# Conditioned layer norm: VectorE reads scale and bias in PSUM, without ScalarE's copies

## What is computed

```python
cond = silu(emb @ f_w1 + f_b1) @ f_w2 + f_b2          # (256, 16), from noise levels
for i in range(4):
    # y = layernorm(x) * (1 + cond @ s1_w[i] + s1_b[i]) + (cond @ b1_w[i] + b1_b[i])
    y = cond_layer_norm(x, cond, s1_w[i], s1_b[i], b1_w[i], b1_b[i])
    x = x + sparse_attention(y, src, dst, wq[i], ..., wo[i], bo[i])
    y = cond_layer_norm(x, cond, s2_w[i], s2_b[i], b2_w[i], b2_b[i])
    x = x + relu(y @ m_w1[i] + m_b1[i]) @ m_w2[i] + m_b2[i]
```

## Time and profile before

| | us |
|---|---|
| median of 3 runs | 902.3 (902.26 to 905.46) |
| the profiled execution, its own time | 895.13 |
| span of its trace | 893.3 |
| PE busy | 777.2 |
| DVE busy | 607.8 |
| ACT busy | 230.4 |
| POOL busy | 139.3 |
| mean granted clock of PE | 0.954 |

### The profile page before, as it was taken

How to read it: one execution, slowest core, us unless ns; L and a number is a source line. 1 busy time by engine, 2 the same in 40 slices (tenths; PEclk the granted TensorE clock), 3 DMA queues, 4 the chain that set the end, 5 groups by cost and what they waited for, 6 DMA issues and landing times.

```text
span 893.3 us, 10417 instructions
## 1 busy us (share of the span) xinstructions
PE 777.2 (87%) x2858; PEld 499.2 (56%) x2858; DVE 607.8 (68%) x1579; ACT 230.4 (26%) x460; POOL 139.3 (16%) x149
## 2 busy tenths in 40 slices
PE   6688898898898999999999997188979995996998
PEld 2345465455466657657558563176566582582673
DVE  8774675675684533533633544288999999999895
ACT  6522122123122321321321221401602403403300
POOL 6000000000001000000010001741261261240000
PEclk9889999999999999999999999599999997997999
DMA  6813214323331333333233100671541452330000
GB/s 203 293 40 114 102 55 150 106 79 121 106 118 40 121 111 113 106 112 112 105 112 107 59 0 23 192 227 51 169 139 47 142 142 71 100 113 0 0 1 23
DMA packets 39653, 89.93 MB, mean 101 GB/s; under 512 B 3986, under 2 KB 4255, under 8 KB 39615
## 3 DMA queue, kind: packets, MB, share of 16 engines
q1 hardware_dynamic: 34496, 72.71, 24.3%
q0 software_dynamic: 5120, 16.78, 6.4%
HBM read 88.43 MB, written 1.05 MB: 100 GB/s over the span
## 4 chain that ended last, share of the span: by engine, by line
PE 33%; issue 32%; DVE 23%; DVEq 7%; POOL 2%; ACT 1%; DMA 1%; POOLq 0%; ACTq 0%; SPq 0%
PE PS L744 23%; DVE big L1446 6%; PE PS L1003 5%; DVE tail L1437 5%; DVEq L1416 3%; DVE tail L1456 2%; DVE prods L1456 2%; PE PS L753 2%; DVEq L1420 1%; POOL rstd L537 1%; DVEq L1446 1%; POOL big L557 1%; DVE h L1088 1%; PE PS L840 1%; PE PS L777 1%
## 5 line engine op out<-in xcount | busy, mean ns | idle before, releaser
L744 PE MATMUL PS<-big 128*128 128x512 f32 (+1 forms) x368 | 137.6, 525 | 2.5 <-DVE big L1350 1.8
L1437 DVE SCALAR_TENSOR_TENSOR tail<-big,coef 128x448 f32 (+3 forms) x216 | 132.3, 615 | 0.0
L1446 DVE TENSOR_TENSOR big<-big,tail 128x448 f32 (+3 forms) x216 | 120.8, 559 | 12.1 <-DVE tail L1437 11.4
L744 PEld LDWEIGHTS PS<-big 128*128 128x128 f32 x368 | 67.3, 190 | 67.0 <-issue 57.9
L537 POOL TENSOR_TENSOR rstd<-var,minus_half 128x1 f32<-128x1 f32 x36 | 29.2, 812 | 439.0 <-DVE var L1062 436.9
L557 POOL DMA_INDIRECT big<-h_rows,src_i x64 | 81.0, 1266 | 82.7 <-PE PS L1003 60.9
L744 PE MATMUL PS<-hT,big 128*128 128x256 f32 x384 | 86.6, 386 | 4.2 <-ACT hT L666 4.2
L744 PEld LDWEIGHTS PS<-hT,big 128*128 128x128 f32 x384 | 73.5, 193 | 16.0 <-issue 3.9
L1003 PE MATMUL PS<-big,hotd_more 128*128 128x512 f32 x176 | 76.5, 592 | 0.0
L1088 DVE TENSOR_TENSOR h<-PS,h 128x512 f32<-128x512 f32 x26 | 17.9, 687 | 74.1 <-PE PS L744 74.1
L1017 PE MATMUL PS<-xn,tail 128*128 128x256 f32 x120 | 32.3, 417 | 33.1 <-DVE tail L1456 33.1
(11 more groups left out here) (196 smaller groups left out, 1074.9 us busy)
## 6 DMA issues: line engine op xcount, KB each, us to landing
big<-in_edge_attr_dram SPq DMA_DIRECT2D x32, 512.0 KB, 3.6
big<-in_L_gnn_vn_W_dram SPq DMA_DIRECT2D x12, 1024.0 KB, 5.3
big<-in_L_gnn_m_w_dram SPq DMA_DIRECT2D x8, 1024.0 KB, 5.2
big<-in_L_gnn_gcn_W_dram SPq DMA_DIRECT2D x7, 1024.0 KB, 5.2
big<-in_L_gnn_wv_dram SPq DMA_DIRECT2D x4, 1024.0 KB, 5.3
big<-in_L_gnn_wq_dram SPq DMA_DIRECT2D x4, 1024.0 KB, 5.4
big<-in_L_gnn_wk_dram SPq DMA_DIRECT2D x4, 1024.0 KB, 5.4
big<-in_L_gnn_wo_dram SPq DMA_DIRECT2D x4, 1024.0 KB, 5.3
```

What stands on the lines that cost most here:

```text
L744: return pe.matmul(o, lhsT, rhs, start=start, stop=stop)
L1437: dve.scalar_tensor_tensor(out=prod[:, slot, tiles, :], in0=xs[:, tiles, bass.ds(i1, EXT)], scalar=coef[:, row:row + 1], in1=xe[:, tiles, ...
L1446: dve.tensor_tensor(o, o, prod[:, slot, tiles, :], ALU.add)._wait_ge(path_step, max(product_at[slot], added_at[0])).then_inc(path_step, 1)
```

## The change

ACT's copies, the tile `tab` and the semaphore `tab_ready` go. DVE waits for PE's `tab_done` and takes its second operand from PSUM. The 1 of the scale comes from an 18th row: the strips are one row longer, row 18 of `condT` is already 1, and POOL fills `tabw` once at the start, the strips of the scale with 1 and those of the bias with 0. SP waits for that before it loads the 17 rows over it.

```diff
-        tab = region(8, 2).rearrange("p (k t n) -> p k t n", k=2, t=NT)
...
         def strip(g):
-            return slice(32 * g, 32 * g + NC + 1)
+            return slice(32 * g, 32 * g + NC + 2)
...
             load_w(4, A["L1_gnn_wk"][0], None)
+            sp.wait_ge(tab_ones, 2)
             load_tab(0, 0)
             load_tab(1, 0)
...
             pool.tensor_scalar(turns, turns, -PI_CLIP, None, ALU.max).then_inc(angle_set, 1)
+            pool.wait_ge(angle_set, 1)
+            pool.memset(tabw[0:2 * 32, :, :], 1.0).then_inc(tab_ones, 1)
+            pool.wait_ge(tab_ones, 1)
+            pool.memset(tabw[2 * 32:4 * 32, :, :], 0.0).then_inc(tab_ones, 1)
+            pool.wait_ge(tab_ones, 2)
...
-            def table(k, t):
-                for part in range(2):
-                    act.wait_ge(tab_done, k * 4 + (2 * t + part + 1))
-                    act.activation(tab[:, part, t, :], PS[:, 4 + 2 * part + t, :], ACT.Identity,
-                                   bias=zero if part else one).then_inc(tab_ready, 1)
...
-                for t in range(NT):
-                    table(b * 2 + 1, t)
                 y_turned(b * 2 + 1, 0)
...
-                if not last:
-                    for t in range(NT):
-                        table(b * 2 + 2, t)
-
-            for t in range(NT):
-                table(0, t)
...
                 dense_T(0, 3, hT, q_done, yT_ready, b * 4)
-                pe.wait_ge(tab_ready, b * 8 + 4)
                 pe.wait_ge(w_in[4], b * 16 + 16)
...
-                dve.wait_ge(tab_ready, k * 4 + (2 * t + 1))
+                dve.wait_ge(tab_done, k * 4 + (2 * t + 1))
                 link(dve.scalar_tensor_tensor(out=xn[:, t, :], in0=h[:, t, :], scalar=mv[:, t, 0:1],
-                                              in1=tab[:, 0, t, :], op0=ALU.subtract, op1=ALU.mult))
+                                              in1=PS[:, 4 + t, :], op0=ALU.subtract, op1=ALU.mult))
                 dve.wait_ge(ln_est, (k + LN_BLOCK) * 2 + (t + 1))
-                dve.wait_ge(tab_ready, k * 4 + (2 * t + 2))
+                dve.wait_ge(tab_done, k * 4 + (2 * t + 2))
                 dve.scalar_tensor_tensor(out=xn[:, t, :], in0=xn[:, t, :], scalar=rstd[:, t:t + 1],
-                                         in1=tab[:, 1, t, :], op0=ALU.mult, op1=ALU.add).then_inc(y_ready, 1)
+                                         in1=PS[:, 6 + t, :], op0=ALU.mult, op1=ALU.add).then_inc(y_ready, 1)
```

More of the change, by code:

```diff
@@ L303, in gnn_stack_kernel @@
                   "rec_est", "z_ready", "conv_done"])
-        tab_done, tab_ready, y_ready, yT_ready, q_done, k_done, v_done, q_ready, k_ready, v_ready = map(
-            sem, ["tab_done", "tab_ready", "y_ready", "yT_ready", "q_done", "k_done", "v_done", "q_ready", "k_ready",
+        tab_done, tab_ones, y_ready, yT_ready, q_done, k_done, v_done, q_ready, k_ready, v_ready = map(
+            sem, ["tab_done", "tab_ones", "y_ready", "yT_ready", "q_done", "k_done", "v_done", "q_ready", "k_ready",
                   "v_ready"])
```

## The result

The changed kernel takes 899.4 us (median of 6 runs, 896.6 to 899.7) against 904.5 us for the kernel before, timed alongside: ratio 0.9942, 95% interval 0.9924 to 0.9959. That is 5.2 us less, between 3.7 and 6.9, where the prediction had 2.6. One of the twelve timed executions of experiment 4 took 4503 us and is left out of its ratio as slow.

The account below looks back on a forecast made before the run. PE, busy 87%, was taken as the bound, with a DVE and POOL chain between products and transposes in the norms. Gains of 3.6 us less 1.0 for memsets gave -2.6: 902.3 to 899.7 us, range 897.5 to 901.5.

Parts of the forecast that it names:

- faster by over 0.5%: Whole kernel: chance 0.26 of a measurable gain, from most of the clock case and the edge of the forecast.
- The copies: ACT, second network: 32 copies of 0.686 us leave, 0 on the path because no engine waits for them.
- The root goes from 1.0 to 0.55: POOL's root in the second network's norms: speeds up to 0.55 us once L1300 beside it reads one operand in PSUM.
- The rival in which the root stays slow: POOL's root gets no faster, only the memsets' +1.0 us remain: 903.3 us; chance 0.14.
- 0.48 us per tile: Norm chain on DVE and POOL: L1304 starts 0.48 us earlier after L1300 in each tile.
- Sites: Second network's norms: 0.9 us at k = 0, 2.2 at k = 2, 4, 6, 0.5 at odd k; together 3.6.
- the forecast's case: Whole kernel as forecast: 897.5 to 901.5 us, from gain 2.3 to 3.9 and memsets 0 to 1.9; chance 0.47.
- PSUM as second operand: L1300 and L1304 on DVE: reading PSUM second costs 0; the skill's estimate was 0.065 us per instruction.
- Memsets: Start of kernel: POOL's two memsets slow DVE's one-hot rows, costing 1.0 us, bounds 0 to 1.9.
- Relief and clock: PE at 270 to 297 us: shorter gaps remove a half-clock stretch, 1.6 us more gain, 897.6 us; chance 0.20.
- The half-rate case: DVE reads SBUF first, PSUM second at half rate: 7.8 us lost, 911.1 us with memsets; chance 0.07.
- given back at the start: Memsets cost their full 1.9 us plus a half-clock stretch of 1.6: sum -0.1, 902.2 us; chance 0.12.

Follow-up runs that it names:

- experiment 4: Kernel before plus only the two POOL memsets and SP's wait for them; ratio to before 1.0016 (1.0004 to 1.0028).
- Experiment 6: Changed kernel with memsets moved ahead of POOL's noise wait, plus 32 unread ACT copies from SBUF at the old places; ratio to before 0.9945.
- experiment 1: Against before: only the scale read in PSUM, ACT still copies the bias (16 copies), 18th row and memsets as in the change; ratio 0.9949.
- experiment 2: Against before: only the bias read in PSUM, ACT still copies the scale, no memsets, 17 rows; ratio 1.0000 (0.9988 to 1.0012).
- Experiment 7: Changed kernel with memsets ahead of POOL's noise wait, and four idle products instead of six at odd k; ratio to before 0.9909, 887.4 us.

## Why the prediction was right

**The number.** 899.7 against 899.4 is closer than the sum deserves. The reference was 902.3 when the sum was carried over (3 runs) and 904.5 in the end (6 runs), and the gain was 5.2 us instead of 2.6; that the two errors cancel is luck. A ratio 0.58% below 1 had a chance of 0.26, as faster by over 0.5%. The mechanism was right, and two terms of the sum were too small, as follows.

**The copies: 0.** Shown. Experiment 6 puts 20.9 us of copies back for 0.02 us.

**The root goes from 1.0 to 0.55 because L1300 no longer reads two tensors in SBUF.** Shown. Experiments 1 and 2 switch one operand each: roots 0.55 and 1.03, ratios 0.9949 and 1.0000. The rule of the Trainium skill ("SBUF — State Buffer", Who interferes with whom) holds here, with 0.48 us as the price for an instruction of 512 columns. The rival in which the root stays slow is out.

**0.48 us per tile.** Exact: 1.35 to 0.87.

**Sites.** Per step between first roots of consecutive norms, experiment 2 (slow roots, full clock) against the changed kernel:

| step from | slow roots | changed | gain | predicted |
|---|---|---|---|---|
| k = 0 | 42.34 | 41.46 | 0.88 | 0.9 |
| k = 2, 4, 6, each | 44.01, 44.01, 43.99 | 43.11, 43.11, 43.08 | 0.90 | 0.73 |
| k = 1, 3, 5, each | 20.98, 20.99, 20.98 | 20.60, 20.61, 20.60 | 0.38 | 0.12 |
| k = 7 | 20.51 | 20.44 | 0.07 | 0.12 |

The sum is 4.80 against 3.6, and above the 3.9 that the prediction gave as its upper end. Two terms were sized too small. At even k the prediction set PE's second half 3.55 us after the first, half of the product's 7.10. L1078 of tile 1 now starts 3.37 us after that of tile 0 (333.42, 336.79), so the second half comes by then at the latest, and tile 0 gives 0.43 us instead of 0.25. It may just bind there: L1078 follows L1294 by 0.71 us where it was 0.67 in the earlier trace rows, in experiment 1 as well. Why the second half comes sooner than half of the modelled length isn't shown. At odd k I took the 0.16 us of idle time that PE shows in the earlier trace rows as all that could be had. The transposes now start 2.60 us after the idle products do (317.62, 320.22), before their modelled end at 2.76, where it was 2.91 us before; that is 0.31 of the 0.38 gained. Experiment 7 shows what the idle products held back: 2.23 us more, 0.56 per site.

**A slip in the bounds.** A gain of 2.3 to 3.9 and memsets of 0 to 1.9 give 898.4 to 901.9 from 902.3, not the 897.5 to 901.5 that the forecast's case states. The measured 899.4 lies in either.

**PSUM as second operand: 0.** Right, 746 and 747 ns. The 62 cycles that the estimate took from the Trainium skill ("VectorE: DVE Perf Modes", The TRN2 errata) are not seen here, neither in duration nor in the next start (0.66 us behind L1302 of experiment 2, 0.67 behind L1304 before).

**Memsets: 1.0 us.** Measured 1.4 (0.4 to 2.5) by experiment 4 against before. By the count stage two memsets cost 1.28 us in the changed kernel (26.63 against 25.35) and 1.42 in experiment 4 (against experiment 2), so the term was too small, inside its bounds of 0 to 1.9: a memset holds the one-hot instruction until it is over. A trace has to be compared with one in which POOL's arithmetic took the same course, as the two courses lie 0.95 us apart. SP's wait was indeed met: its first small load goes at 21.09, the memsets end at 19.93.

**Relief and clock, as a rival.** The stretch of half clock behind k = 0 was absent in the changed kernel, as that case said, but not for its reason: experiments 2 and 4 have the same gaps as before and full clock there. The sum without it is 4.8 - 1.4 = 3.4 us of gain, a little under the 3.7 at the lower end of the measured interval. Whether more of the timed runs of before than of after had such a stretch, the longer count stage or the longer stretch of the third network can't be read from them; that remainder, 1.8 us at the middle of the interval, stays open.

The half-rate case is out by the durations above, and so is "given back at the start".

## What to carry to other kernels

When a small GpSimd instruction stands in a chain, look at what VectorE runs beside it. If that reads two tensors in SBUF, moving one operand to PSUM can shorten the GpSimd instruction, here from 1.03 to 0.55 us, though neither engine's own work changed; whether ScalarE is relieved is beside the point. When a chain gets shorter, fillers that were sized to it become the bound: here trimming them from six to four gave 2.2 us more, and leaving them out cost 6.0 against that, through the clock (both by the distance). And compare distances inside a trace and the granted clock over them before giving a whole difference between two profiles to a change.

## What the runs showed that was not expected

A GpSimd memset of 64x1024 elements (1.0 us) stops VectorE's bf16 one-hot instructions and its int32 conversions until it ends, though it reads nothing: 0.27 us becomes 1.0 to 1.1 us, and 0.71 us are lost per memset. That is more than GpSimd's arithmetic did, beside which the same instructions took 364 ns instead of 269 in the mean. Four of them in a row also left PE with so little work that its clock fell afterwards (0.62 in 24 to 28 us), but no more than 0.5 us of the loss can be put down to that.
